# One-partition codebook, a retimed first row, and two output stores behind a landing

## What is computed

```python
x = x + _L0_ffn_ref(_L0_cond_ref(x, ...), ...)
x = x + _L1_ffn_ref(_L1_cond_ref(x, ..., itok_B_1_7), ...)
```

```python
cb = codebook / jnp.clip(jnp.max(jnp.abs(codebook)), 1e-08)
wg = (weight + lora_delta).reshape(O, I // GROUP, GROUP)
normalized = wg / scale
thresholds = (cb[:-1] + cb[1:]) * 0.5
idx = jnp.searchsorted(thresholds, normalized, side='left')
quantized = cb[idx]
```

## Time and profile before

| | us |
|---|---|
| median of 3 runs | 910.33 |
| lowest and highest | 910.23, 911.14 |
| the profiled execution, its own time | 910.95 |
| its span, first to last instruction | 909.1 |
| TensorE busy, products | 902.2 |
| TensorE busy, weight loads | 787.0 |
| VectorE / ScalarE / GpSimd busy | 616.5 / 313.2 / 144.0 |
| bytes moved | 191.51 MB, mean 211 GB/s |

### The profile page before, as it was taken

The page is one execution under the profiler, slowest core; times in us unless marked ns, Lnnn a source line. Parts: engine busy times, 40 slices in busy tenths (PEclk is TensorE's granted clock), DMA queues, the critical chain, the costliest instruction groups (busy, mean ns, idle before and its releaser), DMA issues.

```text
span 909.1 us, 13369 instructions
## 1 busy us (share of the span) xinstructions
PE 902.2 (99%) x4670; PEld 787.0 (87%) x4670; DVE 616.5 (68%) x1312; ACT 313.2 (34%) x503; POOL 144.0 (16%) x298
## 2 busy tenths in 40 slices
PE   8999999999999999999999999999999999999998
PEld 7999998888998888888888888888888888888886
DVE  6889899865587968976456566566566566566563
ACT  5678778411324433231322222222222222222220
POOL 0100010111001001414213113113113113113110
PEclk9999999999999999999999999999999999999999
DMA  8523330765412033556887887887888887887875
GB/s 340 208 76 122 119 125 24 259 211 166 142 50 94 4 135 94 216 211 225 280 277 258 284 274 262 282 272 263 285 272 266 280 265 270 286 270 263 287 225 184
DMA packets 60540, 191.51 MB, mean 211 GB/s; under 512 B 7965, under 2 KB 10678, under 8 KB 58554
## 3 DMA queue, kind: packets, MB, share of 16 engines
q1 hardware_dynamic: 49610, 159.02, 50.5%
q0 software_dynamic: 10432, 31.35, 11.6%
q10 hardware_dynamic: 432, 0.30, 0.1%
HBM read 158.93 MB, written 32.23 MB: 210 GB/s over the span
## 4 chain that ended last, share of the span: by engine, by line
PE 95%; DMA 4%; SPq 0%; ACT 0%; DVE 0%; issue 0%
PE bank L857 28%; PE bank L519 15%; PE bank L520 15%; PE bank L521 15%; PE bank L840 5%; PE bank L831 5%; DMA t_lo<-t_scratch 3%; PE bank L665 2%; PE bank L905 2%; PE bank L931 2%; PE bank L932 2%; PE bank L933 2%; DMA m_raw<-m1t 1%; PE bank L774 1%; PE bank L580 1%; PE bank L537 0%
## 5 line engine op out<-in xcount | busy, mean ns | idle before, releaser
L857 PE MATMUL bank<-g_hi,xs 128*128 128x512 f32 x448 | 145.2, 395 | 0.0
L857 PE MATMUL bank<-t_hi,xs 128*128 128x512 f32 x336 | 113.3, 396 | 0.3 <-DMA t_lo<-t_scratch 0.2
L490 POOL DMA_DIRECT2D p1sel<-p_scratch x128 | 65.3, 510 | 278.9 <-issue 278.8
L857 PEld LDWEIGHTS bank<-g_hi,xs 128*128 128x128 f32 x448 | 83.3, 188 | 16.3
L857 PE MATMUL bank<-g_lo,xs 128*128 128x512 f32 x224 | 88.3, 394 | 0.0
L977 ACT ACTIVATE xs<-x_raw 128x1024 fp32r<-128x1024 f32 x60 | 61.9, 1056 | 76.1 <-PE bank L857 55.7
L1309 DVE TENSOR_TENSOR xs<-x_raw,xs 128x1024 fp32r<-128x1024 f32 x60 | 75.4, 1279 | 12.0 <-ACT xs L977 11.5
L519 PE MATMUL bank<-gx,xs 128*128 128x304 f32 x256 | 77.5, 303 | 0.0
L521 PE MATMUL bank<-gx,xs 128*128 128x304 f32 x256 | 77.5, 303 | 0.0
L520 PE MATMUL bank<-gx,xs 128*128 128x304 f32 x256 | 77.3, 302 | 0.0
L857 PEld LDWEIGHTS bank<-t_hi,xs 128*128 128x128 f32 x336 | 62.1, 188 | 15.2 <-DMA t_lo<-t_scratch 2.9
(11 more groups left out here) (325 smaller groups left out, 2060.9 us busy)
## 6 DMA issues: line engine op xcount, KB each, us to landing
t_hi<-t_scratch SPq DMA_DIRECT2D x82, 512.0 KB, 4.7
t_lo<-t_scratch SPq DMA_DIRECT2D x82, 512.0 KB, 6.2
x_raw<-xq SPq DMA_DIRECT2D x16, 1024.0 KB, 6.8
out<-ost SPq DMA_DIRECT2D x63, 256.0 KB, 4.3
p1sel<-p_scratch POOLq DMA_DIRECT2D x64, 192.0 KB, 4.4
w_raw<-wall SPq DMA_DIRECT2D x16, 512.0 KB, 4.4
w<-e_scratch SPq DMA_DIRECT2D x6, 1024.0 KB, 5.1
ea<-e_scratch POOLq DMA_DIRECT2D x8, 644.0 KB, 4.5
```

Of the source, the lines that this page charges most:

```text
L490: pool.dma_start(f(p1sel[b][STK * s:STK * s + STK, cs]), p1_dram[bass.ds(i * STK, STK), cs]).then_inc(sems[b], 16)
L857: mm = nc.tensor.matmul(bk[j][:], l[:, c, :], m[:, c, :], start=first and c + k == 0, stop=c + k == KH + 1, skip_group_check=True)
```

## The change

There are three groups of edits.

- **One partition.** The codebook, its thresholds, flags and count and the sequence numbers are loaded and computed on one partition, since all later reads of them take partition 0. Each of the two loads has one descriptor instead of 128.
- **The first row.** 18 products on zeros instead of 15. The low products of chunks 0 and 1 both stand behind the high products of chunk 1, those of chunk 2 behind chunk 3, and so on as before. On VectorE the first three codebook steps stand ahead of the split of chunk 0, the other three behind `w_split(1)`.
- **The stores.** In each of the 14 tiles SyncE waits, ahead of the stores of banks 2 and 1 of the tile before, until both halves of quarter 4 have landed. The order of the issues stays.

The core of the diff (lengths of other rows on one partition are changed in the same way):

```diff
-N_WARM = 15
+N_WARM = 18
...
-        cb = row("cb", [P, LV])
+        cb = row("cb", [1, LV])
...
-            sp.dma_start(idraw[:], ids_b).then_inc(ld_ids, 16)
+            sp.dma_start(idraw[:], ids_r).then_inc(ld_ids, 16)
...
                 load_t(4, 6 * n + 1)
+                for h in range(2):
+                    sp.wait_ge(ld_t[h], 32 * (3 * n + 1))
                 store_out(tau - 1, (2, 1))
                 load_t(3, 6 * n + 3)
...
-                if c == 0:
+                if c == 1:
                     row0_low(0)
-                if c > 1:
+                    row0_low(1)
+                elif c > 2:
                     row0_low(c - 1)
...
-            act.dma_start(cb[:], cbook_b).then_inc(ld_cb, 16)
+            act.dma_start(cb[:], cbook_r).then_inc(ld_cb, 16)
...
+            mag, peak = vcomp[0:1, :], val0[0:1, 0:1]
             v.wait_ge(ws_hi, 1)
             lo_of(w_lo[0][:, 0:2, :], w_raw[0][:, 0:2, :], w_hi[0][:, 0:2, :]).then_inc(ws_lo, 1)
+            v.wait_ge(ld_cb, 16)
+            link(nc.vector.tensor_scalar(mag, cb[:], -1.0, None, ALU.mult))
+            link(nc.vector.tensor_tensor(mag, mag, cb[:], ALU.max))
+            link(nc.vector.reduce_max(peak, mag, AX_X))
             for c in range(KC):
                 m1_split(c)
                 if c == 1:
                     w_split(0)
-                if c > 1:
-                    codebook_scale(c - 2)
             w_split(1)
+            link(nc.vector.tensor_scalar(peak, peak, 1e-8, None, ALU.max))
+            link(nc.vector.reciprocal(peak, peak))
+            link(nc.vector.tensor_scalar(cb[:], cb[:], peak, None, ALU.mult))
             v.wait_ge(ld_pk, 16)
```

More of the change, by code:

```diff
@@ L199, in build @@
         val0 = small("val0", [P, 1])
-        idc = small("idc", [P, T // SEQ], I32)
+        idc = small("idc", [1, T // SEQ], I32)
         bv = small("bv", [P, 12])
@@ L214, in build @@
         tr_at = [tr]
-        cb = row("cb", [P, LV])
-        tt_ = row("tt_", [P, LV + 1])
-        reach = row("reach", [P, LV])
+        cb = row("cb", [1, LV])
+        tt_ = row("tt_", [1, LV + 1])
+        reach = row("reach", [1, LV])
         cols = row("cols", [LV, 4])
@@ L221, in build @@
         valid = row("valid", [P, LV])
-        idraw = row("idraw", [P, T // SEQ], I32)
-        idf = row("idf", [P, T // SEQ])
+        idraw = row("idraw", [1, T // SEQ], I32)
+        idf = row("idf", [1, T // SEQ])
         one1 = row("one1", [P, 1])
@@ L286, in build @@
         st_o = [sem(f"st_o{j}") for j in range(4)]
-        cbook_b = cbook.rearrange("(a n) -> a n", a=1).to_broadcast([P, LV])
-        ids_b = ids.rearrange("(a n) -> a n", a=1).to_broadcast([P, T // SEQ])
+        cbook_r = cbook.rearrange("(a n) -> a n", a=1)
+        ids_r = ids.rearrange("(a n) -> a n", a=1)
         chunked = lambda ap: ap.rearrange("(c p) n -> p c n", p=P)
@@ L1383, in _ @@
                 view = tt_[:, 0:LV].rearrange("p (b w) -> p b w", w=2 * half)
-                mid = view[:, :, half:half + 1].to_broadcast([P, LV // (2 * half), half - 1])
+                mid = view[:, :, half:half + 1].to_broadcast([1, LV // (2 * half), half - 1])
                 nc.vector.tensor_tensor(view[:, :, 1:half], view[:, :, 1:half], mid, ALU.min)
@@ L1390, in _ @@
             link(scale_step(12))
-            nc.vector.reduce_sum(rs2[0][:, 0:1], reach[:], AX_X)
+            nc.vector.reduce_sum(rs2[0][0:1, 0:1], reach[:], AX_X)
             link(scale_step(13))
-            nc.vector.tensor_copy(cnt[:, 0:1], rs2[0][:, 0:1]).then_inc(cols_ok, 1)
+            nc.vector.tensor_copy(cnt[0:1, 0:1], rs2[0][0:1, 0:1]).then_inc(cols_ok, 1)
             v.wait_ge(la_hi_s, 1)
```

## The result

The changed kernel takes 913.81 us (median of 20 runs, 911.39 to 917.54); the kernel before takes 911.10 us beside it (20 runs). The ratio is 1.0032, with a 95% interval of 1.0024 to 1.0039. The time lies in the predicted range and is longer, as was forecast; the 6.2 us more of the forecast are over twice what came. The profiled execution took 914.35 us.

A forecast was written before the change was run, and what follows sets the result against it. TensorE, busy 902.2 of 909.1 us, was taken as the bound. A 0.3 us loss at the start plus 5.9 us in the loop made 6.2 us, so 916.5 us against the median of 910.33; range 912 to 921 us.

The forecast's parts named there:

- Removing the codebook's spread load: At the start: one descriptor instead of 128 lets all later loads come 0.13 us earlier, between 0 and 0.3.
- Row 0 and w_lo: At the start: row 0 ends 0.3 us sooner; the split w_lo and row 1 start 0.39 us sooner.
- The three codebook steps: On VectorE behind w_lo: they take 0.69 us, delaying the thresholds, the count and TensorE's codebook product.
- The start as a whole: Before the tile loop: costs 0.3 us, between a gain of 0.4 and a loss of 0.5 us.
- Three warm-ups, free: At the start on TensorE: three more warm-up products of 0.35 us each cost nothing.
- The new wait puts the stores' data in front of the second quarter: In the tile loop: 1.3 us of store data delays the second quarter's loads, costing 5.9 us more over 14 tiles.
- d: In each tile: the second quarter's delay, the first quarter's last-load lag (issue to landing) minus 6.8 us.
- lower bound of d: In the tile loop: 0.4 us less if stores' data partly fit beside the loads' start; 1.8 us in all.
- What stands behind cannot slow what stands in front: In the DMA queue: removing the stores behind the first quarter's loads brings those loads 0 us, at most 1.1 us.
- Rival 1: In the tile loop: the stores fit the gap before the second quarter; about 911.1 us, chance 0.20.
- Rival 2: In the tile loop: without stores behind it the first quarter lands 0.6 us sooner; 908.8 us, chance 0.13.
- Rival 3: In the tile loop: the delay passes on to the third quarter and the load of x; 921.6 us, chance 0.05.

The follow-up runs named there:

- e8: e1 plus one more load of 128 descriptors, all from the same 256 bytes, right behind the codebook's; 911.54 us, ratio 0.9995 to the kernel before.
- e1: The changed kernel without the wait in front of the stores, so only the start is new; 909.68 us, ratio 0.9985 to the kernel before.
- e11: e1 with the 15 warm-ups and the order of low products of the kernel before; 911.03 us, ratio 0.9990 to the kernel before.
- e2: The kernel before with the wait in front of the two stores as its only edit; 916.08 us, ratio 1.0054 to the kernel before.
- e6: The changed kernel with each moved store writing 256 of its 512 columns; 912.30 us, ratio 0.9991 to the kernel before.
- e7: e1 with each of the two stores, in their old place, writing one row of 128; 909.59 us, ratio 0.9986 to the kernel before.
- e3: e1 with the two stores issued behind the second quarter's loads, without a wait; 914.00 us, ratio 1.0032 to the kernel before.
- e12: e3 a second time: one-row stores were intended, but all 128 rows were stored; 914.08 us, ratio 1.0025 to the kernel before.
- e5: The changed kernel with the stores behind the second quarter's loads, waiting until that quarter has landed; 910.97 us, ratio 0.9997 to the kernel before.
- e10: e1 plus the extra broadcast of e8, issued later, behind ScalarE's two first weight copies; 911.34 us, ratio 0.9995 to the kernel before.
- e9: e1 plus an extra load of 128 descriptors of 256 bytes from 128 different rows; 910.12 us, ratio 0.9988 to the kernel before.

## Why the prediction was right in sign and off in size

- **Removing the codebook's spread load: 0.13 us, between 0 and 0.3.** This step failed. It was priced by its bytes; the broadcast had held the DMA up for about 1.05 us (adding one in e8 moves row 1 by 1.06 us). The rows for it were in the trace of before: a share of 0.59 and 0.81 from 6 to 8 us, when the mean from 12 us on is 1.03.
- **Row 0 and w_lo.** Everything that comes at the DMA's pace is 1.2 to 1.5 us sooner, not 0.3 to 0.4: w_lo at 19.64 (predicted 20.75), row 1 at 21.01 (22.1).
- **The three codebook steps, 0.69 us.** Right: from w_lo's start to the thresholds' it is 1.77 us, before 1.14, so 0.63 us more. The wait at the codebook product was real too. It was half the predicted size (row 1's gain of 1.49 us is 1.21 at the loop, 0.28 lost instead of 0.69), since the chain from the thresholds to the count was 0.17 us shorter on one partition and the handing-on had slack. The start as a whole: -1.4 us by e1 instead of +0.3.
- **Three warm-ups, free.** They cost nothing, as predicted, but e11 and e2 show that they aren't idle filling: without them the clock was still low for row 0 in two of three profiles, and with the new, earlier loads that costs 1.0 us at row 1.
- **The new wait puts the stores' data in front of the second quarter.** Right, place by place: stores 0.04 us behind the landing, loads right behind them, the waits at that quarter (T+20.8 to T+22.5, expected T+20.7), waits up from 2.9 to 7.2 us (expected 8 or more). The loop's cost was 5.9 us by the sum and 4.9 (3.6 to 6.3) by e2, so the two agree within the interval. (Added up again from the 14 pairs of lags, the sum of the waits is 6.7 us and not 6.5, which changes nothing.) The term that measures smaller is d: the sum has the second quarter land later by all of it, 0.7 us on the mean, and it lands 0.5 us later (T+20.3 before, T+20.8 in both after and e2). The stores' data fit in part beside the loads' slow beginning, as the lower bound of d had it: between T+12 and T+13.5 the DMA engines move 146 GB/s before and 240 in the changed kernel, stores and loads together, on the mean of 14 tiles. e6 shows the term that matters, the 1.3 us of data: with half of it away most of the added waits go.
- **What stands behind cannot slow what stands in front.** For the first quarter nearly right (0.13 us, e7), but false as a rule: behind the second quarter the same two stores cost 0.7 us of lag on the mean (e3, e12). It did not carry the forecast, but a cure built on it failed.
- **Rivals.** Rival 1 (the stores fit the gap) is out at its size: the second quarter lands 0.5 us later and seven waits stand where it had three; what fits is the 0.2 us above. Rival 2 (loads land sooner without the stores) has its effect at a quarter of the size, and the packets' 177 against 160 ns show where it acts. The Trainium skill (DMA: Bandwidth & Descriptors, section on latency and other measured facts) says that a lighter HBM load makes a DMA's fixed cost smaller. Here the landing came 0.13 of 7.5 us sooner; that a fixed cost was smaller is not shown. Rival 3 (the delay is passed on) is out for the change: the third quarter lands at T+30.1 after and T+30.6 before, the load of x at T+36.2 and T+36.1. It shows only in e5, where the third quarter's lag was 9.0 us.

The forecast was 6.2 us and 2.7 came: 1.7 us of the difference is the start, 1.0 the loop by e2, and the rest is the spread of the medians.

The best kernel of those that ran is e1, the new start with the stores left in place: 0.15% under the kernel before (0.07 to 0.24%) and 0.47% under the changed one by the two ratios.

## What to carry to other kernels

A wait that keeps stores from behind a load puts them in front of the next one; on a queue that is nearly full in every period, compare the delay with that load's spare time: here 1.3 us of data made it 0.5 us late, and it had 0.2 us to spare. Price a transfer by the hole in the DMA share around its landing, not by its bytes, and look for holes even where the mean is full. A broadcast of one HBM row to all partitions can cost ten times its bytes, so look for its hole, and load one partition instead where there is one and the readers allow it. And before a late load is blamed on its neighbours in the queue, look whether an instruction load fell into it.

## What was not expected of the hardware

- 128 reads of the same 256 bytes in HBM held up the DMA engines for about 1 us (share 0.59 to 0.84 in e8's and before's two microseconds), at the start (e8) and in full queues (e10); 128 reads of different rows did not (e9), nor did 128 reads of one row on SyncE's queue (share 1.06 and 1.03 in the kernel before). Why is not shown.
- Stores that were only queued behind the second quarter's loads lowered the rate from some 400 to 215 to 262 GB/s at a busy share near 1 (e3, e12): a 4 KB packet took 245 to 253 ns instead of 174. Behind the first quarter the same stores made it 177 instead of 160 ns, and stores of one row did not (e7). It happens before the first packet of the stores. Whether their size counts behind the second quarter too, and why the two quarters differ, stays open: the kernel that was to show it did not do so.
- The long landings of the first quarter go with instruction loading. In the kernel before, in the tile where lag4 was 8.2 us and TensorE's weights waited 0.50 us at 480.26, the DMA queues from 476.5 to 480.2 us are (packets, MB, share of 16 engines):

```profile
q1 hardware_dynamic: 448, 1.09, 79.6%
q8 instruction: 1, 0.02, 2.2%
```

2.2% of 16 engines in 3.7 us is 1.3 us on one engine; by the argument, the load's share on that engine had to wait it out. The other tiles bear it out. Before, six of the 14 first quarters have one such packet of 16 KB between their last issue and their landing, and their lag4 is 7.6 to 8.3 us; in the other eight it is 6.7 to 7.4 us. All five waits for that quarter are in the six tiles. Over the 14 profiles 58 of the 61 waits for it are in such tiles, and lag4 is 8.1 us on the mean with such a packet (73 tiles, counted from 2 us ahead of the issue) and 7.1 without (123). Without full stores behind it the lag is 0.2 us shorter in the tiles without the packet and the same in those with it, which is why taking the stores away ended so little of the waiting. No run moves an instruction load, so this is a coincidence in every profile and not yet an experiment.
